# Mixture-of-experts layers in an eight-layer kernel: layer 2's rows dealt over the chunks, layer 1's weight halves issued earlier

## The chip, the cores and the metric

One core of one Trainium2 chip runs the whole program in one launch. The metric is the device time in microseconds (us). A run of this kernel is one execution of it; the time before is given as the median of three runs.

## The reference

Eight residual layers run over x of 8 x 256 tokens of 128 features: four pairs of a cross-attention and a feed-forward layer, each behind a layer norm. Two feed-forward layers matter here, and the text names them as the code does: "layer 1" (L = 3 in the code) and "layer 2" (L = 5).

```python
# layer 1: 64 experts of 88 hidden rows, 8 chosen per token, and a shared one
out = sum_e rw[t, e] * (silu(x @ gw_e.T) * (x @ uw_e.T)) @ dw_e.T
# layer 2: 8 experts, four 128 and four 256 rows wide, 2 chosen per token
probs = sigmoid(xf @ router_w.T)
topw, sel = top_k(probs, 2); topw = topw / (topw.sum(-1) + 1e-20)
h = square(relu(xf @ W1_e)); y_e = h @ W2_e
out = sum_e combine[t, e] * y_e
```

## The kernel before, in words

All 2048 tokens (16 tiles of 128, four groups q of 512) stay in SBUF. Five engines work side by side: PE (TensorE), DVE (VectorE), ACT (ScalarE), POOL (GpSimd), and SP, which only issues loads. Each has its own list of instructions in the order of the code. They wait for one another on semaphores, and a wait holds all that stands behind it on its engine.

**Two halves.** A matrix product of the expert layers runs in the fp32r format, which keeps fewer bits than f32. So every operand is split: ACT copies the f32 value into an fp32r high half, and POOL (or DVE) subtracts it from the f32 value into a low half. A product is then three matmuls (`product`, L1754 through `mm`): high by high, and the two crossed ones.

**Layer 1.** Its 5632 hidden rows are 44 chunks of 128, each with 8 rows of 16 experts. A unit is one chunk for one token group: 176 units. Unit n on PE is `gate_up1(n)` (6 matmuls) and `down1(n-3)` (3 matmuls). ACT does the silu (L1018) and the high half of the hidden rows (L791), DVE the two multiplications (L1552, L1557), POOL the low half (`hidden1_low`, L646). The weights of the next chunk are split once in four units: high halves by ACT (`gate_up1_high` behind s % 4 == 1, `down1_high` behind s % 4 == 2), low halves by POOL (`gate_up1_low` L638 at s % 4 == 2, behind `hidden1_low(s-1)`; `down1_low` L642 at s % 4 == 3). PE waits on `wgu_lo` ahead of the first unit of a chunk. The loads of raw weights wait for the low half that frees their buffer.

**Layer 2.** Its 1536 hidden rows are 12 chunks of 128, each belonging to one expert. The tokens are taken in two halves (hf) of 1024: 12 chunks for two groups, and then the same 12 chunks again, 48 units in all. So the weights of every chunk are split twice. A chunk belongs to a single expert, but each token has its own combine weight for it. PE therefore forms with `rows2` (one bf16 matmul by the selector `sel2` on `cT`, the combine weights split in three bf16 parts) a tile of that weight in PSUM beside each unit. In unit n PE does `up2` (3 matmuls), `rows2` (1) and `down2` (3) of the unit three earlier. ACT does the relu (L1105) and the high half; DVE does u2 = weight row x relu (L1659, PSUM by SBUF), h2 = u2 x relu (L1663, SBUF by SBUF) and the last 128 columns of the low half (L1670, `low2`), POOL the other 384 columns (L682) and the weights' low halves (L673, L677).

**Ahead of layer 2's units** PE forms the router's logits behind the transposes of the normed tokens. ACT takes the sigmoid (L1090) and then writes the high halves of the tokens (`norm_high`), POOL their low halves (`norm_low`, L614). DVE first does `integer_weights` (for the last layer), then finds every expert's rank among 8 by comparing all pairs (`rank_of`, L1483 to L1487, on 1024 elements), masks, normalises and splits the weights (L1642 to L1653). PE transposes them (L2226), ACT copies the result to `cT`. **Behind the units** ACT waits for all `down2`, copies the four sums (`o2T`), PE transposes them (L2268), and DVE adds them to X (L1275) and starts the next norm.

## Time and profile before

| what | value |
| --- | --- |
| median of three runs | 1149.82 us (1143.99, 1149.82, 1149.83) |
| the profiled execution's own time | 1143.57 us |
| its span, first to last instruction | 1141.8 us |
| mean granted TensorE clock | 0.921 |
| DMA, whole span | 23.02 MB, 20 GB/s on average |
| chain that ended last, by engine | PE 66%, DVE 19%, POOL 7%, issue 4%, ACT 4% |

The granted clock is 1.0 at 2.4 GHz and 0.5 at 1.2 GHz. Loads are small and far from any limit. PE carries most of the chain, but the eight layers have different limits, so each stretch is read by itself: layer 1's units run from about 450 to 818 us of the span, layer 2's routing from 882 to 898 us, and its units from 899 to 1012 us.

### The profile page before, as it was taken

To read this page: it belongs to the slowest core of one execution; us is meant where nothing else is said; L and a number is where in the kernel's file an instruction comes from. 1 tells how busy PE (TensorE), PEld (TensorE's weight loads), DVE (VectorE), ACT (ScalarE), POOL (GpSimd) and SP (SyncE) were. 2 spreads that over 40 slices of the span, in tenths; PEclk is the share of its full clock that TensorE was granted. 3 is DMA by queue.
4 is the path that set the end of the run, shared out by engine and by line. 5 is a ranking of instruction groups with operands and counts; after the bars stand their busy time and mean duration, and the time that the engine had idled before them with its cause. 6 is when DMAs were issued, how large, how long until landed. Compare 5 with 4: busy or idle time off the path is not lost.

```text
span 1141.8 us, 16173 instructions
## 1 busy us (share of the span) xinstructions
PE 974.2 (85%) x4525; PEld 716.0 (63%) x4525; DVE 778.8 (68%) x1598; ACT 584.3 (51%) x1145; POOL 536.4 (47%) x544
## 2 busy tenths in 40 slices
PE   5799899989998886999999999999966687857465
PEld 3577566657677644877777777777646444435244
DVE  7676455555534686666666666667568899976896
ACT  2344566665532254665656656566413455532584
POOL 6011322223303002777777777777555688763300
PEclk9899899999999898999999999999976699989576
DMA  5000000003200000000000000000010000000001
GB/s 166 1 1 1 1 1 1 1 25 101 78 10 24 1 1 12 24 22 28 21 24 25 21 25 23 21 28 21 0 61 1 1 1 0 1 0 1 0 8 30
DMA packets 27107, 23.02 MB, mean 20 GB/s; under 512 B 3419, under 2 KB 24115, under 8 KB 26931
## 3 DMA queue, kind: packets, MB, share of 16 engines
q1 hardware_dynamic: 27059, 22.43, 6.7%
q8 instruction: 24, 0.39, 0.1%
q14 instruction: 24, 0.20, 0.1%
HBM read 21.37 MB, written 1.05 MB: 20 GB/s over the span
## 4 chain that ended last, share of the span: by engine, by line
PE 66%; DVE 19%; POOL 7%; issue 4%; ACT 4%; DMA 0%; SPq 0%; POOLq 0%; ACTq 0%; DVEq 0%
PE psum L1754 59%; POOL hh L682 2%; DVE stats L1231 1%; PE psum L1875 1%; DVE xn L1244 1%; PE psum L1883 1%; DVE arena L1663 1%; PE psum L1823 1%; POOL rstd L594 1%; POOL wgu L673 1%; DVE arena L1307 1%; POOL xall L614 1%; POOL wdn L677 1%; DVE arena L1659 1%; DVE mv L1234 1%
## 5 line engine op out<-in xcount | busy, mean ns | idle before, releaser
L1754 PE MATMUL psum<-xall,wgu 128*128 128x512 f32 x1424 | 394.5, 411 | 27.6 <-POOL wgu L673 11.1
L1754 PEld LDWEIGHTS psum<-xall,wgu 128*128 128x128 f32 x1424 | 268.9, 193 | 114.0 <-issue 49.8
L646 POOL TENSOR_TENSOR hh<-arena,hh 128x512 fp32r<-128x512 f32 x176 | 227.7, 1294 | 107.1 <-ACT hh L791 105.0
L1754 PE MATMUL psum<-hh,wdn 128*128 128x512 f32 x672 | 197.0, 402 | 22.1 <-DVE hh L1670 22.1
L1552 DVE TENSOR_TENSOR psum<-psum,arena 128x512 f32<-128x512 f32 x176 | 123.0, 699 | 111.0 <-PE psum L1754 102.3
L1018 ACT ACTIVATE arena<-psum 128x512 f32<-128x512 f32 x176 | 105.3, 598 | 143.5 <-PE psum L1754 143.5
L791 ACT ACTIVATE hh<-arena 128x512 fp32r<-128x512 f32 x224 | 140.7, 628 | 50.9 <-DVE arena L1663 47.5
L1754 PEld LDWEIGHTS psum<-hh,wdn 128*128 128x128 f32 x672 | 123.6, 190 | 60.0 <-DVE hh L1670 23.3
L1754 PE MATMUL psum<-arena 128*128 128x18 f32 (+7 forms) x816 | 137.0, 318 | 5.7 <-DVE X L1634 3.5
L1557 DVE TENSOR_TENSOR arena<-psum,arena 128x512 f32<-128x512 f32 x176 | 121.7, 691 | 7.5 <-DVE psum L1552 1.7
L791 ACT ACTIVATE arena<-psum 128x1024 f32<-128x1024 f32 (+8 forms) x114 | 77.4, 691 | 96.4 <-PE psum L1754 31.9
L1754 PEld LDWEIGHTS psum<-arena 128*128 128x128 f32 (+3 forms) x816 | 97.5, 186 | 30.5 <-issue 26.6
L594 POOL TENSOR_TENSOR rstd<-veps,neghalf 128x4 f32<-128x4 f32 x24 | 24.3, 1014 | 108.4 <-DVE veps L1237 108.1
L747 POOL TENSOR_TENSOR arena<-arena 128x512 f32<-128x512 f32 x32 | 33.3, 1041 | 83.7 <-DVE arena L1359 83.6
L682 POOL TENSOR_TENSOR hh<-arena,hh 128x384 fp32r<-128x384 f32 x48 | 49.4, 1028 | 23.3 <-ACT hh L791 23.2
L1663 DVE TENSOR_TENSOR arena<-arena 128x512 f32<-128x512 f32 x48 | 57.2, 1191 | 3.4 <-DVE arena L1659 2.1
L618 POOL TENSOR_TENSOR wgu<-egu,wgu 128x256 fp32r<-128x256 f32 x32 | 24.0, 751 | 56.6 <-ACT wgu L791 56.6
L1772 PE MATMUL psum<-ident,xn 128*128 128x128 f32 x112 | 26.5, 396 | 26.5 <-POOL xn L600 13.5
L1404 DVE SCALAR_TENSOR_TENSOR arena<-psum,ebias,arena 128x512 f32<-128x512 f32 x32 | 24.0, 751 | 32.6 <-PE psum L1754 31.6
L638 POOL TENSOR_TENSOR wgu<-egu,wgu 128x256 fp32r<-128x256 f32 x44 | 32.8, 746 | 28.2 <-DVE arena L1533 28.2
L791 ACT ACTIVATE xnT<-psum 128x512 f32<-128x512 f32 x24 | 14.3, 598 | 57.2 <-PE psum L1772 57.1
L859 ACT ACTIVATE arena<-psum,arena 128x256 f32<-128x256 f32 x64 | 29.8, 470 | 25.1 <-DVE arena L1352 24.3
(287 smaller groups left out, 1493.9 us busy)
## 6 DMA issues: line engine op xcount, KB each, us to landing
egu<-in_w SPq DMA_DIRECT2D x44, 128.0 KB, 2.0
egu<-in_egu SPq DMA_DIRECT2D x16, 256.0 KB, 2.8
edn<-in_w SPq DMA_DIRECT2D x44, 64.0 KB, 1.8
edn<-in_edn SPq DMA_DIRECT2D x16, 128.0 KB, 2.0
arena<-in_w SPq DMA_DIRECT2D x1, 1536.0 KB, 5.9
X<-in_x SPq DMA_DIRECT2D x4, 256.0 KB, 3.8
out<-X SPq DMA_DIRECT2D x4, 256.0 KB, 2.3
arena<-in_ctxTd SPq DMA_DIRECT2D x1, 512.0 KB, 5.1
```

Of the source, the lines that this page charges most:

```text
L594: pool.tensor_tensor(rstd[:, s], veps[:, s], neghalf[:, s], ALU.pow).then_inc(ln_rstd, 1)
L638: pool.tensor_tensor(wgu[:, slot, 1, :], w1gu(slot), wgu[:, slot, 0, :].bitcast(F32), ALU.subtract).then_inc(wgu_lo, 1)
L646: pool.tensor_tensor(hh[:, s % 4, 1, :], h1[:, s % 2, :], hh[:, s % 4, 0, :].bitcast(F32), ALU.subtract).then_inc(hh_lo, 1)
L682: pool.tensor_tensor(hidden2_part(k, 1)[:, r], h2[:, k % 2, r], hidden2_part(k, 0)[:, r].bitcast(F32), ALU.subtract).then_inc(hh_lo, 1)
L747: pool.tensor_tensor(qb[:, k % 2], qb[:, k % 2], wide(recB[:, k % 2].unsqueeze(2), 2, N), ALU.mult)\
L791: return act.activation(dst, src, ACT.Copy)
L859: last = act.activation(qb[:, k % 2, c, :], psum[:, k % 2, c * N:(c + 1) * N], ACT.Exp, bias=nmB[:, k % 2, c:c + 1], accum_out=sumB[:, k % ...
L1018: act.activation(sil[:, k, :], bank(k), ACT.Silu).then_inc(nl_done, 1)
L1552: dve.tensor_tensor(bank(2 + k), bank(2 + k), sil[:, k, :], ALU.mult).then_inc(prod_done, 1)
L1557: dve.tensor_tensor(h1[:, k, :], bank(2 + k), rwb[:, s // 4, own], ALU.mult).then_inc(hid_done, 1)
L1663: dve.tensor_tensor(h2[:, k, :], u2[:, k, :], r2[:, k, :], ALU.mult).then_inc(hid_done, 1)
L1754: return pe.matmul(dst, lhsT=lhsT, rhs=rhs, start=start, stop=stop)
```

## The change: what it does

- **Layer 1.** ACT's `gate_up1_high` moves from behind s % 4 == 1 to behind s % 4 == 0; POOL's `gate_up1_low` moves from s % 4 == 2, behind `hidden1_low`, to s % 4 == 1, ahead of `hidden1_low`. The halves for the down product stay where they are.
- **Layer 2's rows** are dealt anew when the weights are laid out on the host: chunks 0 to 3 hold 32 rows of each of the four narrow experts, chunks 4 to 11 hold 32 rows of each of the four broad ones. So there are only two different tiles of combine weights over all tokens (`cB`). They are made once, by 8 matmuls and 8 copies; `rows2` goes.
- **All four token groups** pass through a chunk, in straight code in place of loops: 48 units again, but each chunk's weights are split once.
- **The hidden rows** take two scalar_tensor_tensor instructions on DVE, each with the unit's PSUM tile as one input: v2w = max(up, 0) x cB, h2 = max(up, 0) x v2w. ACT's relu and DVE's `low2` go; POOL makes all 512 columns of the low half. DVE does `weighted2(n+1)` ahead of `hidden2(n)`. In `down2` the matmul that needs the low half comes last, with a wait of its own.
- **Routing** uses max and match_replace, 16 of each, in place of the pairwise ranks; `integer_weights` comes behind it. The tokens' low halves go from POOL to DVE (`norm_low`, from PSUM), their high halves to just behind each group's transposes. Four groups of `up2` stand ahead of the combine weights on PE.
- **The end**: ACT copies a group's sum as soon as that group's last `down2` is done. Also, the selector tile shrinks from 12 to 2, a memset on POOL and a second load of chunk 0 go.

The core of the diff (`NC2` is 12, `NG` 4, `UNITS2` 48):

```diff
         taken[0] = 0
         pr2 = carve(NT, E2)
-        g2a = carve(NT, 8, 8)
-        g2b = carve(NT, 8, 8)
-        rank2 = carve(NT, 8)
+        best2 = carve(NT, 8)
+        rest2 = carve(NT, E2)
+        cw2 = carve(NT, E2)
         rs2 = carve(2, NT)
-        cpk = carve(NT, P, dt=BF16)
+        cpk = carve(NT, 3 * E2, dt=BF16)
         cT = carve(T, dt=BF16)
-        r2 = carve(2, 512)
-        u2 = carve(2, 512)
+        cB = carve(2, T)
+        v2w = carve(3, 512)
         h2 = carve(2, 512)
         o2T = carve(T)
...
                 def chunk_group(j, last=False):
                     for s in range(4 * RG):
+                        ahead = s // 4 + 1
+                        weights = not (last and ahead == RG)
+                        if s % 4 == 1 and weights:
+                            gate_up1_low(j * RG + ahead, ahead % 2)
                         if later(j, 1) or s:
                             hidden1_low(j * (4 * RG) + (s - 1), s - 1)
-                        ahead = s // 4 + 1
-                        if last and ahead == RG:
-                            continue
-                        if s % 4 == 2:
-                            gate_up1_low(j * RG + ahead, ahead % 2)
-                        if s % 4 == 3:
+                        if s % 4 == 3 and weights:
                             down1_low(j * RG + ahead, ahead % 2)
...
+            def hidden2_low(n):
+                pool.wait_ge(hh_hi, DONE1 + n + 1)
+                pool.tensor_tensor(hh[:, n % 4, 1, :], h2[:, n % 2, :], hh[:, n % 4, 0, :].bitcast(F32), ALU.subtract).then_inc(hh_lo, 1)
...
+                for c in range(2):
+                    up2_low(c)
+                    down2_low(c)
+                for n in range(UNITS2):
+                    c, s = n // NG, n % NG
+                    hidden2_low(n)
+                    if 1 <= c < NC2 - 1:
+                        if s == 0:
+                            up2_low(c + 1)
+                        if s == 2:
+                            down2_low(c + 1)
...
                     if later(j, 1) or s >= 2:
                         silu1(j * (4 * RG) + s, s % 2)
+                    ahead = s // 4 + 1
+                    weights = not (last and ahead == RG)
                     if later(j, 1) or s:
                         hidden1_high(j * (4 * RG) + (s - 1), s - 1)
-                    ahead = s // 4 + 1
-                    if last and ahead == RG:
-                        continue
-                    if s % 4 == 1:
+                    if s % 4 == 0 and weights:
                         gate_up1_high(j * RG + ahead, ahead % 2, j * (8 * RG) + (8 * E0 + 16 * (ahead // 2) + 16))
-                    if s % 4 == 2:
+                    if s % 4 == 2 and weights:
                         down1_high(j * RG + ahead, ahead % 2, j * (8 * RG) + (8 * E0 + 16 * (ahead // 2) + 16))
...
-            ln_evac(5)
+            for g in range(NG):
+                r = slice(512 * g, 512 * g + 512)
+                act.wait_ge(ln_tp, NG * 5 + g + 1)
+                copy(xnT[:, r], bank(LN_BANKS[5][g])).then_inc(ln_xnT, 1)
+                copy(norm_half(g, 0), bank(LN_BANKS[5][g])).then_inc(xh_hi, 1)
...
+            for k in range(4):
+                act.wait_ge(rb_mm, NG * RG + 2 * k + 1)
+                copy(cB[:, k // 2, 1024 * (k % 2):1024 * (k % 2) + 512], bank(4 + 2 * (k % 2))).then_inc(rb_sb[0], 1)
+            for n in range(UNITS2):
+                c, s = n // NG, n % NG
+                hidden2_high(n)
+                if 1 <= c < NC2 - 1:
+                    if s == 0:
+                        up2_high(c + 1)
+                    if s == 2:
+                        down2_high(c + 1)
             for q in range(NG):
+                act.wait_ge(down_done, DONE1 + UNITS2 - NG + q + 1)
...
+            for g in range(NG):
+                norm_low(5, g)
+            dve.wait_ge(rl_sig, 3)
+            for t in range(NT):
+                last = dve.max(best2[:, t, :], pr2[:, t, :])
+            then(last)
+            dve.tensor_tensor(rs2[:, 0, :], best2[:, :, 0], best2[:, :, 1], ALU.add)
+            then(dve.memset(best2[:, :, 2:8], 3.0e38))
+            dve.tensor_scalar(rs2[:, 0, :], rs2[:, 0, :], 1e-20, None, ALU.add)
+            for t in range(NT):
+                last = dve.match_replace(rest2[:, t, :], best2[:, t, :], pr2[:, t, :], -3.0e38)
+            then(last)
+            dve.tensor_tensor(rest2, pr2, rest2, ALU.not_equal)
+            then(dve.reciprocal(rs2[:, 1, :], rs2[:, 0, :]))
+            then(dve.tensor_tensor(cw2, rest2, pr2, ALU.mult))
+            then(dve.tensor_tensor(cw2, cw2, wide(rs2[:, 1, :].unsqueeze(2), NT, E2), ALU.mult))
+            then(dve.tensor_copy(cpk[:, :, 0:E2], cw2))
+            then(dve.tensor_tensor(cw2, cw2, cpk[:, :, 0:E2], ALU.subtract))
+            then(dve.tensor_copy(cpk[:, :, E2:2 * E2], cw2))
+            then(dve.tensor_tensor(cw2, cw2, cpk[:, :, E2:2 * E2], ALU.subtract))
+            dve.tensor_copy(cpk[:, :, 2 * E2:3 * E2], cw2).then_inc(rw_done, 1)
             integer_weights()
-            dve.wait_ge(rl_sig, 3)
...
-            def hidden2(n, s, first):
-
-                k = s % 2
-                dve.wait_ge(nl_done, n + 1)
-                dve.tensor_tensor(u2[:, k, :], bank(2 + k), r2[:, k, :], ALU.mult).then_inc(prod_done, 1)
-                dve.wait_ge(prod_done, n + 1)
-                dve.wait_ge(hh_hi, n - 1)
-                dve.wait_ge(hh_lo, n - 1)
-                dve.tensor_tensor(h2[:, k, :], u2[:, k, :], r2[:, k, :], ALU.mult).then_inc(hid_done, 1)
-                if not first:
-                    low2(n - 1, (s - 1) % 4)
-
-            def low2(n, k):
-                r = slice(LOW2, 512)
-                dve.wait_ge(hh_hi, n + 1)
-                dve.tensor_tensor(hidden2_part(k, 1)[:, r], h2[:, k % 2, r], hidden2_part(k, 0)[:, r].bitcast(F32), ALU.subtract).then_inc(hh_lo2, 1)
...
+            for k in range(4):
+                dve.wait_ge(rb_mm, NG * RG + 2 * k + 2)
+                dve.tensor_copy(cB[:, k // 2, 1024 * (k % 2) + 512:1024 * (k % 2) + 1024], bank(5 + 2 * (k % 2))).then_inc(rb_sb[1], 1)
+            for k in range(2):
+                dve.wait_ge(rb_sb[k], 2 * RG + 4)
+
+            def weighted2(n):
+                dve.wait_ge(up_ready, DONE1 + n + 1)
+                if n >= 3:
+                    dve.wait_ge(hid_done, DONE1 + n - 2)
+                q = n % NG
+                dve.scalar_tensor_tensor(v2w[:, n % 3, :], bank(q), 0.0, cB[:, 0 if n < 4 * NG else 1, 512 * q:512 * q + 512], ALU.max, ALU.mult)\
+                    .then_inc(prod_done, 1)
+
+            def hidden2(n):
+                dve.wait_ge(prod_done, DONE1 + n + 1)
+                if n >= 2:
+                    dve.wait_ge(hh_hi, DONE1 + n - 1)
+                    dve.wait_ge(hh_lo, DONE1 + n - 1)
+                dve.scalar_tensor_tensor(h2[:, n % 2, :], bank(n % NG), 0.0, v2w[:, n % 3, :], ALU.max, ALU.mult).then_inc(hid_done, 1)
+
+            weighted2(0)
+            for n in range(UNITS2):
+                if n + 1 < UNITS2:
+                    weighted2(n + 1)
+                hidden2(n)
             output_groups(6, NG)
...
-            def rows2(local, k, hf):
-
-                mm(bank(2 + k), sel2[:, bass.ds(local, 1), :].rearrange("p a n -> p (a n)"),
-                   cT[:, 1024 * hf + 512 * k:1024 * hf + 512 * k + 512]).then_inc(up_ready, 1)
...
+            def up2(n):
+                c, q = n // NG, n % NG
+                if q == 0:
+                    pe.wait_ge(wgu_lo, STEPS0 + NC1 + c + 1)
+                if n >= 4:
+                    pe.wait_ge(hid_done, DONE1 + n - 3)
+                else:
+                    pe.wait_ge(xh_lo, E0 + NG + q + 1)
+                if n == 0:
+                    pe.wait_ge(rl_sig, 3)
+                product(bank(q), lambda h: wgu[:, c % 2, h, 0:P], lambda h: norm_half(q, h)).then_inc(up_ready, 1)
+
+            def down2(n):
+                c, q = n // NG, n % NG
+                if q == 0:
+                    pe.wait_ge(wdn_lo, NC1 + c + 1)
+                pe.wait_ge(hh_hi, DONE1 + n + 1)
+                mm(bank(4 + q), wdn[:, c % 2, 1, :], hh[:, n % 4, 0, :], c == 0, False)
+                mm(bank(4 + q), wdn[:, c % 2, 0, :], hh[:, n % 4, 0, :], False, False)
+                pe.wait_ge(hh_lo, DONE1 + n + 1)
+                mm(bank(4 + q), wdn[:, c % 2, 0, :], hh[:, n % 4, 1, :], False, c == NC2 - 1).then_inc(down_done, 1)
+
...
+                for k in range(2 * NG):
+                    e, q = k // NG, k % NG
+                    if e:
+                        pe.wait_ge(rb_sb[q % 2], 2 * RG + q // 2 + 1)
+                    mm(bank(4 + q), sel2[0:3 * E2, e, :], cT[0:3 * E2, 512 * q:512 * q + 512]).then_inc(rb_mm, 1)
+                for q in range(2):
+                    pe.wait_ge(rb_sb[q], 2 * RG + 4)
+
+            for n in range(UNITS2 + 3):
+                if n < UNITS2:
+                    up2(n)
+                if n == 3:
+                    combine_rows2()
+                if n >= 3:
+                    down2(n - 3)
             for g in range(NG):
...
+    narrow = np.arange(4 * 128).reshape(4, 4, P // 4).transpose(1, 0, 2)
+    broad = 4 * 128 + np.arange(4 * 256).reshape(4, 8, P // 4).transpose(1, 0, 2)
+    dealt = np.concatenate([narrow.reshape(-1), broad.reshape(-1)])
+    w2 = np.concatenate([v["L2_ffn_w1"][:, dealt].reshape(D, NC2, P).transpose(1, 0, 2), v["L2_ffn_w2"][dealt].reshape(NC2, P, D)], axis=2).transpose(1, 0, 2)
```

## Rows read from the trace of the kernel before

**Rows 1.** The page: busy time of each engine over the span.
```profile
PE 974.2 (85%) x4525; PEld 716.0 (63%) x4525; DVE 778.8 (68%) x1598; ACT 584.3 (51%) x1145; POOL 536.4 (47%) x544
```
**Rows 2.** Windows view: start:end, length, busy us of each engine (instructions), granted clock, DMA.
```profile
455.00:816.00 361.00, 361.00 (x1544) 286.24 (x1544) 243.42 (x350) 217.62 (x427) 271.11 (x257) 1.00 0.08 23
...
899.00:1012.00 113.00, 90.17 (x326) 54.76 (x327) 107.98 (x144) 62.46 (x142) 88.56 (x95) 0.97 0.00 1
```
**Rows 3.** Timeline of PE, layer 1: start, us, line, operation, count.
```profile
560.04 1.52 PE L1754 MATMUL psum<-xall,wgu 128*128 128x512 f32 x6
...
562.08 1.52 PE L1754 MATMUL psum<-xall,wgu 128*128 128x512 f32 x6
...
564.25 1.65 PE L1754 MATMUL psum<-xall,wgu 128*128 128x512 f32 x6
...
572.68 0.49 PE L1754 MATMUL psum<-xall,wgu 128*128 128x512 f32 x1
```
**Rows 4.** Timeline of all engines, layer 1, around 564 us.
```profile
563.37 0.75 POOL L638 TENSOR_TENSOR wgu<-egu,wgu 128x256 fp32r<-128x256 f32 x1
```
**Rows 5.** Timeline, start of layer 1's second chunk; in brackets the idle time before it.
```profile
454.81 0.50 PE L1754 MATMUL psum<-xall,wgu 128*128 128x512 f32 x1 [0.99 <-POOL wgu L638]
```
**Rows 6.** Groups by shape, 900 to 1010 us (layer 2): busy us, mean ns, idle before.
```profile
L1663 DVE TENSOR_TENSOR arena<-arena 128x512 f32<-128x512 f32 x48 | 57.2, 1191 | 3.4 <-DVE arena L1659 2.1
L682 POOL TENSOR_TENSOR hh<-arena,hh 128x384 fp32r<-128x384 f32 x47 | 48.2, 1026 | 22.0 <-ACT hh L791 21.9
...
L1659 DVE TENSOR_TENSOR arena<-psum,arena 128x512 f32<-128x512 f32 x47 | 31.9, 678 | 0.0
...
L1670 DVE TENSOR_TENSOR hh<-arena,hh 128x128 fp32r<-128x128 f32 x47 | 25.3, 539 | 0.0
```
**Rows 7.** Groups by shape, 500 to 800 us (layer 1).
```profile
L646 POOL TENSOR_TENSOR hh<-arena,hh 128x512 fp32r<-128x512 f32 x143 | 185.1, 1294 | 76.1 <-ACT hh L791 74.6
...
L1552 DVE TENSOR_TENSOR psum<-psum,arena 128x512 f32<-128x512 f32 x143 | 100.0, 699 | 93.8 <-PE psum L1754 86.3 <-ACT arena L1018 7.5
...
L791 ACT ACTIVATE hh<-arena 128x512 fp32r<-128x512 f32 x143 | 89.7, 627 | 0.0
...
L642 POOL TENSOR_TENSOR wdn<-edn,wdn 128x128 fp32r<-128x128 f32 x35 | 16.8, 480 | 0.0
```
**Rows 8.** Two lines with scalar_tensor_tensor, by source: ns min/median/max, first and last start.
```profile
L1404 DVE SCALAR_TENSOR_TENSOR arena<-psum,ebias,arena x32: 749/751/754, 248.9 to 323.2; 128x512 f32<-128x512 f32 x32
...
L1705 DVE SCALAR_TENSOR_TENSOR arena<-arena,cols x16: 751/752/1411, 1071.6 to 1116.9; 128x512 f32<-128x512 f32 x16
```
**Rows 9.** Timeline of all engines, layer 2's routing.
```profile
881.78 0.28 ACT L1090 ACTIVATE arena<-psum 128x128 f32<-128x128 f32 x1 [2.67 <-PE psum L1754]
...
891.72 2.90 PE L1754 MATMUL psum<-xall,wgu 128*128 128x512 f32 x6 [10.03 <-POOL wgu L673]
...
893.90 0.29 DVE L1652 TENSOR_TENSOR arena<-arena 128x128 f32<-128x128 f32 x1
...
894.51 1.89 PE L2226 MATMUL psum<-identb,arena 128*128 128x128 bf16 x16
895.58 1.94 ACT L791 ACTIVATE arena<-psum 128x1024 bf16<-128x1024 bf16 x2 [11.24 <-PE psum L2226]
...
898.85 0.69 DVE L1659 TENSOR_TENSOR arena<-psum,arena 128x512 f32<-128x512 f32 x1 [4.40 <-ACT arena L1105]
```
**Rows 10.** Timeline of DVE, layer 1's routing.
```profile
416.67 1.19 DVE L1510 MAX8 arena<-arena 128x8 f32<-128x8 f32 x16
...
418.08 0.09 DVE L1514 MATCH_VALUE_LOAD arena<-arena 128x8 f32 x1
...
420.19 0.15 DVE L1514 MATCH_REPLACE8 arena<-arena 128x8 f32<-128x8 f32 x1
```
**Rows 11.** Timeline of all engines, end of layer 2's units.
```profile
1010.62 1.11 POOL L682 TENSOR_TENSOR hh<-arena,hh 128x384 fp32r<-128x384 f32 x1 [1.29 <-ACT hh L791]
...
1014.89 0.69 DVE L1275 TENSOR_TENSOR X<-psum,X 128x512 f32<-128x512 f32 x1 [4.02 <-PE psum L2268]
```

More of the change, by code:

```diff
@@ L1476, in _ @@
                 norm_behind(3, t)
-            def rank_of(dst, v, a, b2, n):
-                own = wide(v.unsqueeze(3), n, 8, 8)
-                other = wide(v.unsqueeze(2), n, 8, 8)
-                dve.tensor_tensor(b2, other, own, ALU.is_equal)
-                then(dve.tensor_tensor(a, other, own, ALU.is_gt))
-                then(dve.tensor_tensor(b2, b2, wide(ltmask[:, :, :].unsqueeze(1), n, 8, 8), ALU.mult))
-                then(dve.tensor_tensor(a, a, b2, ALU.add))
-                then(dve.tensor_reduce(dst, a, AX.X, ALU.add))
             def routing():
@@ L1763, in ln_transpose @@
                 pe.wait_ge(ln_xn, NG * L + g + 1)
-                if g >= 2:
+                into = LN_BANKS[L][g] if L in LN_BANKS else 6 + g % 2
+                if g >= 2 and L not in LN_BANKS:
                     pe.wait_ge(ln_xnT, NG * L + g - 1)
```

223 lines of the change are left out of this document (51 added, 172 removed).

## The prediction

> **What bounds the kernel now.** I read the page first: PE is busy 85% of the span, DVE 68% [rows 1]. That is an average over eight layers, so the windows view comes next, one window per stretch that the change touches. In layer 1's units PE is busy 361.00 of 361 us: PE is the bound. In layer 2's units it is DVE, busy 107.98 of 113 us, with PE at 90.17 and the clock at 0.97 [rows 2].
>
> Then the two stretches from near. In layer 1 a unit of nine matmuls usually takes 562.08 - 560.04 = 2.04 us, 0.227 us each. From 564.25 to 572.68 are four units: 8.43 us, where four times 2.04 are 8.16. The first unit of a chunk is late: it starts at 564.25, where 562.08 + 2.04 is 564.12 [rows 3]. POOL's low half of that chunk's weights ended at 563.37 + 0.75 = 564.12 [rows 4]. So PE waits for it, and loses 0.13 us in the wait and as much again in the matmuls behind it. In layer 2, DVE's three instructions per unit take 0.68 + 1.19 + 0.54 = 2.41 us, overlapping a little: 48 units need 112 us. Two of the three have both inputs in SBUF; the 512-column one takes 1.19 us, while the one that reads PSUM takes 0.68 for as many columns [rows 6]. DVE is what orders the unit: PE and ACT wait for it.
>
> **Layer 1, the weight halves.** The instructions are the same; only their places change. ACT issues the high half one unit sooner, and POOL issues the low half ahead of a hidden half instead of behind it and one unit sooner, so it ends about two units (4 us) before PE wants it. What could be late next is that hidden half: it now stands behind 0.75 us of weights. But those come while ACT's high half of the hidden rows isn't there yet, and POOL sits idle 76.1 of 300 us waiting for it [rows 7]; PE uses it three units later. The reload of the raw weights is freed earlier too, no later. So all of 8.43 - 8.16 = 0.27 us goes, at 42 chunk starts: 11 us. At the second chunk, PE's idle 0.99 us for the same weights goes too [rows 5]. Sum: **-12 us**; at the least 0 (the wait moves), at the most 12.5.
>
> **Layer 2, one unit after.** PE: 6 matmuls, 6 x 0.227 = 1.36 us. DVE: two scalar_tensor_tensor on 512 columns with a PSUM input. This form with an immediate scalar isn't in the trace. Its bounds are the tensor_tensor with a PSUM input, 0.70 [rows 7], and the scalar_tensor_tensor with a pointer scalar, 0.75 [rows 8]. So 1.40 to 1.50 us. ACT: 0.63 for the high half [rows 7], and small weight copies. POOL: 1.29 for 512 columns, and per chunk two weight halves at 0.48 [rows 7]: (4 x 1.29 + 2 x 0.48)/4 = 1.53 us. I don't take the slower POOL price of now (1.03 for 384 columns; the weights' 128 columns too are slower beside DVE's SBUF by SBUF instructions [rows 6]): line 646 has one duration throughout, next to DVE instructions that read PSUM.
>
> The engines are then close together, so the loop of waits counts. Say POOL ends low(n-3) at 0. The last matmul of down2(n-3) can start 0.23 later: in rows 3 and 4 that's the time from POOL's end to the first matmul that runs at the usual spacing (564.12 to 564.35). Then `up2(n+1)` has to follow in PE's order: three steps of 0.227, and 0.43 from the last start to the DVE start (a matmul's 0.39 and the semaphore): 1.34. DVE: weighted2(n+1) takes 0.65 until hidden2(n) starts, and that ends 0.70 later: 2.69. ACT 0.04 + 0.63, POOL 0.07 + 1.29: low(n) ends at 4.72. That is three units: 1.57 us each. With one weight half and one hidden half of POOL in the loop it is (4.72 + 1.29 + 0.48)/4 = 1.62; with DVE at 0.75 an eighth of a microsecond more goes into each round, 1.65. I take **1.64 us per unit**. Ends: 1.53 (POOL alone) and 1.80 (each of some three hand-overs per round slower by 0.15 us).
>
> **Layer 2, ahead of the units.** Now 17.1 us pass from the sigmoid at 881.78 to DVE's first unit at 898.85 [rows 9]. After: DVE's four token low halves (4 x 0.69 = 2.8 us) stand ahead of the sigmoid in the place of `integer_weights`, six instructions of the same width; the sigmoid's time is set by PE's router matmuls. From 882.1: 16 max 1.2 us; match_replace 0.137 us per tile (418.08 to 420.34 for 16), 2.3 us [rows 10]; some twelve small instructions at about 0.3 [rows 9] 3.4 us. The weights are ready at 888.9, where they now are at 894.5. `integer_weights` lies behind that, under PE's transposes and ACT's copies. The transposes and ACT's copies stay: 894.51 to 897.52, 3.0 us [rows 9], so `cT` stands at 892. New: 8 broadcast matmuls and 8 copies, four each on ACT and DVE, which alternate at 0.65 us: about 4 us with the first matmul at the low clock. DVE's first unit comes at 896.1: **-2.7 us**. PE meanwhile does up2 of four groups, 12 matmuls at 0.43 (six took 2.90 [rows 9]), 5.1 us from about 883 on: hidden.
>
> **The units.** Now: 898.85 to POOL's last half at 1011.73 [rows 9, 11], 112.9 us. After: low(0) ends 4.1 us behind DVE's first instruction; 46 units at 1.64 are 75.4; the last, with nothing behind it, 1.3; and 1.5 for matmuls at the lower clock until PE is warm, as now. Sum 82.3: **-30.6 us**. **The end:** now 3.16 us from POOL's last half to the first add into X [rows 11]. After, three of the four sums are already copied: some 1.3, **-1.9 us**. POOL's shorter selector and the memset that goes lie where it waits: 0.
>
> **Sum.** 12 + 2.7 + 30.6 + 1.9 = 47.2 us less. Against the profiled execution's own time, 1143.57: 1096.4 us. Of the three runs, one lies next to that time and two 6 us above it, so I put the forecast a little higher, at **1098 us**.
>
> **A rule against a measurement.** Of DVE beside POOL the rows say this: scalar_tensor_tensor with a PSUM input took 749 to 754 ns in all 32 cases, and the one with two SBUF inputs took 1411 once, against 752 [rows 8]; that once lay beside a POOL instruction. The Trainium skill (SBUF — State Buffer, "Who interferes with whom") says that a DVE instruction with at most one SBUF input doesn't contend with GpSimd, and one with two does when GpSimd reads SBUF. By that rule, the trace agrees. The skill's page on VectorE: DVE Perf Modes, on the other hand, gives an fp32 tensor_tensor (N + 151)/0.96, 691 ns here; with that for the new form as an estimate, the unit would come to 1.62.
>
> **Rivals.**
> - *PE loses its clock* (chance 0.04). PE would now pause in every round for POOL's half. At 0.427 us per matmul a unit costs 6 x 0.427 = 2.56 us, 48 x 0.92 = 44 us more than I forecast: 1142 us, no change. Against it: now PE pauses more (80% busy) and the clock stays up [rows 2]. The Trainium skill (TensorE: Matmul & The Clock Gate) tells of a kernel whose short idle times between groups of matmuls made the clock oscillate; here the granted clock doesn't show that.
> - *Layer 1's stall only moves* (0.08), say to the hidden half behind the weights: 1098 + 11 = 1109 us. For it: POOL has four instructions in a row there. Against it: POOL's idle time and the three units of distance.
> - *The loop in layer 2 is slower* (0.10): double-buffered `h2` and a semaphore at each step; with 2.0 us a unit 1098 + 47 x 0.36 = 1115 us.
> - *DVE and POOL exclude each other* (0.02), the one that ends slower. Each unit would cost 1.45 + 1.53 = 2.98 us, 48 x 1.34 = 64 us more: 1162 us, against 1143.6. It decides from about 2.8 us a unit on: then the loss of 48 x 0.47 = 22 us eats the 16.6 us won elsewhere and 5.7 more. Against it: rows 7 and 8.
> - *The change doesn't do what it says* (0.01): some wait keeps layer 2's groups in the old order; 1131 us from layer 1 alone.
>
> **How the numbers follow.** The forecast has 0.75. Its own range is 1.53 to 1.80 us a unit, -5 to +8 us, with 6 us of difference between runs: 1090 to 1110. With the next two rivals it reaches to 1115; below, DVE and PE in full step and layer 2's routing 3 us shorter give 1086. Range 1086 to 1115. A measurement of this kernel tells about 0.5% (5.7 us) from no change. Faster by more than that: 0.95; within it: 0.03, the clock's case; slower: 0.02.
>
> **What would show it.** In the profile after, layer 1's chunk takes 8.16 us, with no wait for the weights' low half. Layer 2's units take 79 us instead of 113, DVE's two lines 0.70 to 0.75 us each, POOL's low half 1.29, and DVE is busy about 88%, POOL 93%. PE's wait in `down2` is for POOL's half. The granted clock stays at 1.0. I am wrong if the unit takes over 1.8 us, if DVE's instructions are over 0.8 us, or if layer 1 keeps its 8.43.

## The result and the profile after

The kernel after takes **1088.83 us** (median of 4 runs, 1087.94 to 1094.18); the kernel before, on the same chip, 1146.90 (4 runs, 1141.13 to 1149.83). The ratio is 0.951, 95% interval 0.947 to 0.956: faster by 5%. The forecast was 1098, range 1086 to 1115. The profiled execution of after took 1088.47 us (span 1086.3), against 1143.57 (span 1141.8) before: 55.1 us less, where the sum of the prediction had 47.2.

I divided both spans at the same events and took the differences (us). "Product" in the table is the first of DVE's two multiplications of a layer 1 unit (L1552 before, L1499 after), not a matrix product; "last half" is the end of POOL's last low half.

| stage | before | after | difference | predicted |
|---|---|---|---|---|
| layer 1, first to last product | 367.38 | 354.84 | -12.54 | -12 |
| last product to first add into X | 12.11 | 12.08 | 0 | 0 |
| first add into X to attention's first add | 32.33 | 30.83 | -1.5 | 0 |
| attention's first add to the sigmoid | 20.69 | 19.62 | -1.1 | 0 |
| sigmoid to DVE's first unit of layer 2 | 17.07 | 13.76 | -3.3 | -2.7 |
| layer 2's units, to POOL's last half | 112.88 | 78.53 | -34.35 | -30.6 |
| POOL's last half to the first add into X | 3.16 | 1.11 | -2.05 | -1.9 |
| from there to the end | 126.92 | 127.15 | +0.2 | 0 |

Layer 1's first product came 0.9 us earlier as well, which no part of the change touches; in the profiles of this kernel and its variants it comes anywhere between 447.8 and 452.1 us. So single runs are compared by stages below, not by their totals.

The page of after, busy time and instructions of each engine (before: [rows 1]):

```profile
PE 950.2 (87%) x4485; PEld 716.7 (66%) x4485; DVE 728.9 (67%) x1602; ACT 557.3 (51%) x1077; POOL 502.8 (46%) x512
```
The windows of after over layer 1's units and within layer 2's (before: [rows 2]):

```profile
450.00:812.00 362.00, 360.26 (x1575) 295.52 (x1576) 249.54 (x358) 222.31 (x436) 276.23 (x261) 1.00 0.08 23
890.00:955.00 65.00, 64.21 (x246) 42.67 (x244) 53.07 (x83) 29.90 (x61) 61.27 (x62) 1.00 0.00 1
```
Layer 1 is still PE's. In layer 2 DVE, which was busy 96% and set the unit, is now at 82% (53.07 of 65); POOL is at 94% and PE at 99%. The forecast had 88% for DVE and 93% for POOL.

Layer 1, timeline of PE and POOL after, where chunks start at 550.70 and 558.86 (before: [rows 3] and [rows 4]):

```profile
548.66 1.52 PE L1710 MATMUL psum<-xall,wgu 128*128 128x512 f32 x6
...
550.70 1.52 PE L1710 MATMUL psum<-xall,wgu 128*128 128x512 f32 x6
...
558.86 1.52 PE L1710 MATMUL psum<-xall,wgu 128*128 128x512 f32 x6
```
```profile
545.94 0.75 POOL L624 TENSOR_TENSOR wgu<-egu,wgu 128x256 fp32r<-128x256 f32 x1
546.65 1.29 POOL L632 TENSOR_TENSOR hh<-arena,hh 128x512 fp32r<-128x512 f32 x1
...
554.03 0.75 POOL L624 TENSOR_TENSOR wgu<-egu,wgu 128x256 fp32r<-128x256 f32 x1
```
Every unit is 2.04 us after the last, the first of a chunk too: 550.70 - 548.66 = 2.04 and 558.86 - 550.70 = 8.16. The low half ends at 546.69, 4.0 us or two units ahead of its use at 550.70; the hidden half stands right behind it, and makes nobody wait.

Layer 2, groups by shape from 890 to 955 us of after (before: [rows 6]), and the waits of the same stretch (who waits for whom: us in total, times, longest):

```profile
L666 POOL TENSOR_TENSOR hh<-arena,hh 128x512 fp32r<-128x512 f32 x42 | 54.4, 1295 | 4.3 <-ACT hh L762 3.6
L1627 DVE SCALAR_TENSOR_TENSOR arena<-psum,arena 128x512 f32<-128x512 f32 x42 | 28.6, 681 | 0.2 <-DVE arena L1619 0.2
L1619 DVE SCALAR_TENSOR_TENSOR arena<-psum,arena 128x512 f32<-128x512 f32 x41 | 28.4, 692 | 11.5 <-PE psum L1710 11.0
...
L658 POOL TENSOR_TENSOR wgu<-arena,wgu 128x128 fp32r<-128x128 f32 x10 | 4.6, 462 | 0.0
```
```profile
ACT hh L762 <- DVE arena L1627: 35.5, 42, 1.1
PEld psum L1710 <- POOL hh L666: 12.4, 40, 0.6
DVE arena L1619 <- PE psum L1710: 11.0, 36, 0.6
POOL hh L666 <- ACT hh L762: 3.6, 17, 0.6
```
Read the waits as a ring. In nearly every unit PE's weight load for the last matmul of `down2` waits for POOL, DVE for PE, ACT for DVE; POOL waits for ACT in 17 of 42. The unit is 1.574 us long (mean of 32, from the ninth start of line 1619 on). Of that POOL works (4 x 1.295 + 2 x 0.462)/4 = 1.53 us, DVE 1.37, and PE's six matmuls of 0.227 need 1.36. PE's busy time shows more: the ends of matmuls are modelled in this profile, and one of `down2` is given 421 ns on the mean, one of layer 1 389.

The routing after (before: [rows 9]), timeline:

```profile
865.73 0.28 ACT L1060 ACTIVATE arena<-psum 128x128 f32<-128x128 f32 x1 [2.19 <-PE psum L1710]
...
866.04 1.19 DVE L1590 MAX8 arena<-arena 128x8 f32<-128x8 f32 x16 [1.77 <-ACT arena L1060]
...
872.60 0.23 DVE L1606 CAST arena<-arena 128x128 bf16<-128x128 f32 x1
...
873.54 1.92 ACT L762 ACTIVATE arena<-psum 24x1024 bf16<-24x1024 bf16 x2 [6.74 <-PE psum L2184]
...
879.49 1.29 DVE L1619 SCALAR_TENSOR_TENSOR arena<-psum,arena 128x512 f32<-128x512 f32 x2
```
The weights are ready 7.1 us behind the sigmoid (forecast 7.1), `cT` 9.7 (10.2), DVE's first unit 13.8 (14.3).

### The profile page after: what moved, and what is told of

It reads as the page before. It is cut to its first block, busy times and chain, and to the rows that moved or that the text cites. A ratio compares the mean times of both kernels' runs of the same rounds, so it can differ in the third digit from the quotient of the medians.

```text
span 1086.3 us, 15531 instructions
## 1 busy us (share of the span) xinstructions
PE 950.2 (87%) x4485; PEld 716.7 (66%) x4485; DVE 728.9 (67%) x1602; ACT 557.3 (51%) x1077; POOL 502.8 (46%) x512
## 4 chain that ended last, share of the span: by engine, by line
PE 73%; DVE 17%; POOL 3%; ACT 3%; issue 2%; DMA 0%; SPq 0%; DVEq 0%; ACTq 0%
PE psum L1710 66%; DVE stats L1189 1%; PE psum L1832 1%; PE psum L1840 1%; PE psum L1780 1%; POOL rstd L586 1%; DVE xn L1202 1%; DVE arena L1265 1%; POOL hh L666 1%; PE psum L1729 1%; DVE mv L1192 1%; PE psum L1903 1%; DVE arena L1660 1%; DVE arena L1661 1%; DVE arena L1667 1%
## 5 line engine op out<-in xcount | busy, mean ns | idle before, releaser
L1710 PEld LDWEIGHTS psum<-xall,wgu 128*128 128x128 f32 x1424 | 272.7, 194 | 88.2 <-issue 25.6
L632 POOL TENSOR_TENSOR hh<-arena,hh 128x512 fp32r<-128x512 f32 x176 | 227.9, 1295 | 81.4 <-ACT hh L762 80.1
L1499 DVE TENSOR_TENSOR psum<-psum,arena 128x512 f32<-128x512 f32 x176 | 123.0, 699 | 98.4 <-PE psum L1710 92.1
L1710 PEld LDWEIGHTS psum<-hh,wdn 128*128 128x128 f32 x672 | 126.5, 189 | 45.9 <-POOL hh L666 16.1
L1710 PE MATMUL psum<-arena 128*128 128x18 f32 (+7 forms) x776 | 122.0, 317 | 5.3 <-DVE X L1581 2.6
L762 ACT ACTIVATE arena<-psum 128x1024 f32<-128x1024 f32 (+9 forms) x118 | 79.7, 687 | 90.4 <-PE psum L1710 30.1
L1710 PEld LDWEIGHTS psum<-arena 128*128 128x128 f32 (+3 forms) x776 | 95.0, 193 | 18.8 <-issue 14.8
L666 POOL TENSOR_TENSOR hh<-arena,hh 128x512 fp32r<-128x512 f32 x48 | 61.9, 1293 | 20.4 <-ACT hh L762 19.7
L1619 DVE SCALAR_TENSOR_TENSOR arena<-psum,arena 128x512 f32<-128x512 f32 x48 | 33.1, 691 | 13.6 <-PE psum L1710 12.9
L762 ACT ACTIVATE xnT<-psum 128x512 f32<-128x512 f32 x24 | 14.3, 598 | 53.4 <-PE psum L1729 53.3
```

The costliest lines, as they stand in the source:

```text
L632: pool.tensor_tensor(hh[:, s % 4, 1, :], h1[:, s % 2, :], hh[:, s % 4, 0, :].bitcast(F32), ALU.subtract).then_inc(hh_lo, 1)
L666: pool.tensor_tensor(hh[:, n % 4, 1, :], h2[:, n % 2, :], hh[:, n % 4, 0, :].bitcast(F32), ALU.subtract).then_inc(hh_lo, 1)
L762: return act.activation(dst, src, ACT.Copy)
L1499: dve.tensor_tensor(bank(2 + k), bank(2 + k), sil[:, k, :], ALU.mult).then_inc(prod_done, 1)
L1619: dve.scalar_tensor_tensor(v2w[:, n % 3, :], bank(q), 0.0, cB[:, 0 if n < 4 * NG else 1, 512 * q:512 * q + 512], ALU.max, ALU.mult)\
L1710: return pe.matmul(dst, lhsT=lhsT, rhs=rhs, start=start, stop=stop)
```

## Experiments

**Layer 1's part alone.** The kernel before, with two orders changed:

```diff
+                        if s % 4 == 1 and weights:
+                            gate_up1_low(j * RG + ahead, ahead % 2)
                         if later(j, 1) or s:
                             hidden1_low(j * (4 * RG) + (s - 1), s - 1)
-                        if s % 4 == 2:
-                            gate_up1_low(j * RG + ahead, ahead % 2)
...
-                    if s % 4 == 1:
+                    if s % 4 == 0 and weights:
                         gate_up1_high(...)
```


> The kernel before with only layer 1's two orders changed (ACT's and POOL's weight halves one unit sooner, POOL's ahead of the hidden half); layer 2 as before. My theory (the 0.27 us at each chunk start go, and nothing else of layer 1 is touched): layer 1 from its first product to its last takes 354.8 us instead of 367.4, a chunk 8.16 instead of 8.43, layer 2's stages keep their times, and the run is 12.5 us shorter than the kernel before (ratio 0.989). Rival (a part of layer 1's gain depends on what else changed, the rest moves to a later wait): a chunk over 8.2 us or a gain under 10 us.

Measured: 1131.26 us (4 runs) against 1142.17, ratio 0.989 (0.984 to 0.993). That is under 2%, but clear of no change. Layer 1 takes 354.82 us, a chunk 8.16. The other stages of the table keep their times within 0.6 us; what lies ahead of layer 1's first product, where nothing was changed, was 2.8 us longer in the profiled run. The gain is layer 1's and needs nothing else.

**Only ACT's half of it.** `if s % 4 == 1` becomes `if s % 4 == 0` for the high half on ACT; POOL's order stays.

> The kernel before with only ACT's high half of layer 1's gate and up weights one unit sooner; POOL's low half stays where it was, behind the hidden half. My theory (what is late is POOL's low half by its place in POOL's order, not for want of its input): POOL's instruction starts where it did, and a chunk keeps 8.43 us; the gain is under 1 us. Rival (ACT's place was what held it): 8.16 us and 12 us less.

Measured: one run, 1143.91 us; layer 1 takes 367.35 us. POOL's low half and PE's next unit, in the timelines of POOL and of PE, and then, from the kernel before, ACT's high half of the same chunk's weights:

```profile
563.66 0.75 POOL L638 TENSOR_TENSOR wgu<-egu,wgu 128x256 fp32r<-128x256 f32 x1
```
```profile
562.37 1.52 PE L1754 MATMUL psum<-xall,wgu 128*128 128x512 f32 x6
...
564.54 1.65 PE L1754 MATMUL psum<-xall,wgu 128*128 128x512 f32 x6
```
```profile
559.90 0.41 ACT L791 ACTIVATE wgu<-egu 128x256 fp32r<-128x256 f32 x1
```
POOL ends at 564.41, PE starts 0.13 us behind it and 2.17 behind its unit before: the pattern of [rows 3] and [rows 4]. So ACT's move by itself gains nothing. In the kernel before, ACT's half was ready at 560.31, and POOL began its own at 563.37 [rows 4], straight behind a hidden half: what held it was its place in POOL's order. Whether POOL's move alone, with ACT's left out, would have won all 12.5 us no run shows; by these times POOL's input would have been there in time.

**POOL's removed work given back.** After, plus the old selector and the old memset on tiles that nobody reads:

```diff
+                    then(pool.memset(idle_sel, 0.0))
+                    for part in range(3):
+                        then(pool.affine_select(out=idle_sel[:, 0:4, :], ...))
+                        then(pool.affine_select(out=idle_wide, ...))
...
+                    pool.memset(idle_pk, 0.0).then_inc(pool_step, 1)
                     experts2_low()
```


> The changed kernel with the work that POOL no longer does given back, on tiles that nobody reads: the memset of 128 x 1536 and the six selections of the old selector ahead of layer 2's attention, and the memset of 128 x 2048 after it. The prediction priced their removal at 0. By it: no stage changes. By the theory formed from the two profiles (DVE's layer-norm instructions run slower while POOL writes memory beside them): the stage from layer 1's first add into X to attention's first takes 32.3 us again instead of 30.8, attention's first add to the sigmoid 20.7 instead of 19.6, the eight layer-norm instructions there 4.4 us instead of 2.5 and the four 2.4 instead of 1.1; together 2.6 us more. Layer 2's units keep 1.57 us each.

Measured: one run, 1090.39 us. The two stages take 31.82 and 20.69 us: +1.0 and +1.1. DVE's layer-norm line of after, then the same line with POOL's work beside it, then that work and the second stretch again by single instructions (ns: least, median, most; in after 336, 339, 345):

```profile
825.03 2.50 DVE L1202 TENSOR_SCALAR xn<-X,mv,rstd 128x128 f32<-128x128 f32 x8 [0.98 <-POOL rstd L586]
859.94 1.11 DVE L1202 TENSOR_SCALAR xn<-X,mv,rstd 128x128 f32<-128x128 f32 x4 [1.12 <-POOL rstd L586]
```
```profile
825.96 4.39 DVE L1214 TENSOR_SCALAR xn<-X,mv,rstd 128x128 f32<-128x128 f32 x8 [0.98 <-POOL rstd L589]
861.87 2.37 DVE L1214 TENSOR_SCALAR xn<-X,mv,rstd 128x128 f32<-128x128 f32 x4 [1.12 <-POOL rstd L589]
```
```profile
826.85 1.38 POOL L745 MEMSET arena<- 128x1536 bf16 x1
...
861.78 1.80 POOL L763 MEMSET arena<- 128x2048 bf16 x1
```
```profile
L1214 DVE TENSOR_SCALAR xn<-X,mv,rstd x4: 329/968/1796, 861.9 to 863.9; 128x128 f32<-128x128 f32 x4
```
These are DVE instructions with one SBUF tensor as input, and a memset reads nothing. They don't all get slower: of the four in the second stretch, the two that begin while the memset runs last until it ends, 1.80 and 1.60 us instead of 0.34, and the other two keep their time. In the first stretch the memset holds two so (1.57 and 1.38 us), and the selections behind it two more (0.80 and 1.08). So 2.1 us of the 2.6 unforeseen in these two stages are this; the other 0.5 us also went with layer 1's part alone (31.79 instead of 32.33), where POOL's work is the old one. I did not isolate it; the granted clock rose and fell at other moments of that stage in the two.

**The pairwise ranking given back.** After, with `rank_of` and its masks in place of max and match_replace.

> The changed kernel with the old pairwise comparison of the eight experts in place of max and match_replace; the order of the work around it, the masks and the units stay new. In the profile before, the weights were ready 12.4 us behind DVE's start on them (882.09 to 894.45), five wide instructions taking 9.1 of it; after the change 6.8 us (866.04 to 872.83). My theory (the routing gains by its fewer and smaller instructions, and pays for it with the broadcast rows): the stage from the sigmoid to DVE's first unit is 5.6 us longer, 19.3 us instead of 13.8, the run that much slower. Rival (before, POOL's token halves beside them slowed these five, which read two SBUF inputs; without POOL there they take their short times): 1.2 us each, only 2 to 3 us longer.

Measured: one run, 1094.65 us; sigmoid to DVE's first unit 17.5 us, +3.8: between the two. Its third wide instruction and a POOL instruction that it met; then, from the kernel before, the same instruction at 2.17 us and POOL's work beside it:

```profile
870.78 1.44 POOL L665 TENSOR_TENSOR wdn<-arena,wdn 128x128 fp32r<-128x128 f32 x1
871.93 1.37 DVE L1446 TENSOR_TENSOR arena<-arena,ltmask 128x1024 f32<-128x1024 f32 x1
```
```profile
882.66 8.39 POOL L614 TENSOR_TENSOR xall<-xnT,xall 128x512 fp32r<-128x512 f32 x4 [6.00 <-ACT xall L791]
...
885.56 2.17 DVE L1485 TENSOR_TENSOR arena<-arena,ltmask 128x1024 f32<-128x1024 f32 x1
```
The five wide instructions take 6.7 us here and took 9.1 before. POOL's small weight halves beside them wait in turn: four took 1.23 to 1.44 us instead of 0.46. So some 2.4 us of the routing's gain came from moving the token halves off POOL and 3.8 from the new instructions; of these 6.2 the stage kept 3.3, and the rest went into what the change adds there, the broadcast rows above all: from `cT` to DVE's first unit 4.0 us pass after, and 1.3 before.

**What sets layer 2's unit: four kernels.** First `down2` one unit later in PE's order (`range(UNITS2 + 4)`, `if n >= 4: down2(n - 4)`).

> The changed kernel with down2 one unit later in PE's order (up2(n), then down2(n - 4) instead of n - 3). My theory (the unit of 1.57 us is set by the loop low(n-3), down2, up2(n+1), weighted2, hidden2, ACT, low(n): 4.7 us for three units): the loop now spans four units, 1.18 us each, and POOL's own work remains: (4 x 1.295 + 2 x 0.462)/4 = 1.53 us, POOL busy all of it; 1.7 us less in all. Rival 1 (POOL alone sets the unit already and 1.57 is its work with small gaps): 1.57 stays. Rival 2 (the waits of DVE on POOL through the two hidden buffers set it): 1.57 stays too, but POOL still has gaps behind ACT's copies.

Then the kernel after with POOL's low halves of the weights left out from the third chunk on; PE waits for `wgu_hi` and `wdn_hi` there and multiplies by the low halves of an earlier chunk, so this kernel serves for its times only.

> The changed kernel without POOL's low halves of layer 2's weights from the third chunk on (PE multiplies by the halves of two chunks earlier there; it waits for ACT's high halves instead). POOL's work falls from 1.53 to 1.30 us per unit. My theory (three units of lag: a loop of 4.6 us through POOL, PE, DVE, ACT and POOL again): the unit falls only to 1.54 us, at the least 1.47 (the time that two of the four units of a chunk have now). Rival (POOL's own work is the bound of the unit): 1.30 to 1.36 us, layer 2's units 10 us shorter.

And both:

> Both: down2 one unit later, and no low halves of the weights on POOL from the third chunk on. In the run with the later down2 the unit was 1.544 us, POOL's work 1.53. My theory: with both bounds moved the next is the pair of hidden buffers, hidden2(n) behind POOL's low(n-2): 0.07 + 0.69 + 0.04 + 0.63 + 0.07 + 1.30 = 2.80 us for two units, 1.40 us, beside DVE's own 1.37; so 1.40 to 1.43. Rival (PE: six matmuls of 0.227 are 1.36, and loads not hidden add to them): PE busy all the time and a unit over 1.45.

| kernel | POOL's own work | unit | DVE's first unit to POOL's last half |
|---|---|---|---|
| after | 1.53 | 1.574 | 78.53 |
| down2 later | 1.53 | 1.544 | 75.73 |
| no low weights | 1.30 | 1.532 | 77.11 |
| both | 1.30 | 1.436 | 71.87 |

POOL's share of work fell by 0.23 us and the unit by 0.04: POOL alone was no bound. With one more unit between the halves the unit meets POOL's own work, (4 x 1.301 + 2 x 0.462)/4 = 1.53, and POOL's waits for ACT nearly vanish. The two bounds lie 0.04 us apart, so moving one alone shortens the stage by 2.8 or 1.4 us, and moving both by 6.7. The waits of the three variants from 890 to 950 us, in that order, show the bound moving:

```profile
PEld psum L1710 <- POOL wgu L658: 7.7, 9, 0.9
...
POOL hh L666 <- ACT hh L762: 1.1, 5, 0.3
```
```profile
PEld psum L1705 <- POOL hh L666: 12.2, 38, 0.6
DVE arena L1614 <- PE psum L1705: 8.1, 25, 0.5
```
```profile
POOL hh L666 <- ACT hh L757: 6.2, 22, 0.6
DVE arena L1622 <- POOL hh L666: 5.6, 16, 0.9
```
In the second the ring of after is left as it was (PE for POOL in 38 units). In the third DVE waits for POOL through the two hidden buffers, as expected; its unit, 1.436, lies just above the 1.40 to 1.43 that this theory gave. These kernels tell what bounds the unit of after. What the single parts of the change are worth in layer 2 (the rows dealt anew, fewer instructions on DVE) they don't tell; no run gives the dealing of the rows back.

**The operands decide, not the form.** `hidden2` reads `v2w` twice instead of `bank(n % NG)` and `v2w`; it computes something else, and serves for its times only.

> The changed kernel with hidden2 reading the weighted hidden twice, from SBUF, instead of once from SBUF and once from PSUM (so the product isn't the reference's); sizes, waits and engines stay. It measures the rival that DVE and POOL exclude each other, which the change avoids by reading PSUM. By that rule DVE's instruction takes 1.2 to 1.4 us instead of 0.68 (rows of before: 1.19 mean beside POOL, 1.41 once), POOL's low half up to as much longer, and the unit 1.9 to 2.3 us instead of 1.57: 16 to 35 us more. If it isn't the operands but the instruction's form that decides, 0.68 and 1.57 stay.

Measured: one run, 1112.90 us; the unit is 2.066 us. Groups from 890 to 950 us, and DVE's line by single instructions over all units (ns: least, median, most):

```profile
L666 POOL TENSOR_TENSOR hh<-arena,hh 128x512 fp32r<-128x512 f32 x30 | 42.6, 1440 | 7.2 <-ACT hh L762 7.2
L1627 DVE SCALAR_TENSOR_TENSOR arena<-arena 128x512 f32<-128x512 f32 x30 | 34.7, 1156 | 8.6 <-POOL hh L666 8.6
```
```profile
L1627 DVE SCALAR_TENSOR_TENSOR arena<-arena x48: 673/994/1665, 881.8 to 978.4; 128x512 f32<-128x512 f32 x48
```
681 ns became 1156 on the mean by where one operand lies, and POOL's instruction grew from 1295 to 1440. The means hide two cases. The 24 of these instructions that begin while no POOL instruction runs take 0.67 or 0.68 us, as with PSUM; the 24 that begin while one runs take 1.31 to 1.66. So two SBUF inputs cost DVE nothing by themselves. The units and their end take 23.7 us more: a good half of what the change wins in layer 2 hangs on each unit instruction having one SBUF input.

**A better version, in two steps.** With POOL's work and the ring both in the way, POOL makes all low weight halves ahead of the units, ACT copies both halves at once, `down2` comes one unit later and `h2` has three buffers:

```diff
+    pool.tensor_tensor(w2x[:, a:b, 1, :], w2all[:, a:b, :], w2x[:, a:b, 0, :], ALU.subtract).then_inc(w2_lo, 1)
...
+    copy(wgu[:, c % 2, :, 0:P], w2x[:, c, :, 0:P]).then_inc(wgu_lo, 1)
+    copy(wdn[:, c % 2, :, :], w2x[:, c, :, P:2 * P]).then_inc(wdn_lo, 1)
```


> A version that may beat both: POOL makes the low halves of all twelve chunks' weights while DVE does layer 2's routing (seven instructions, 8 us, where POOL waits now); in the units ACT copies both halves of a chunk in one instruction; down2 one unit later; three hidden buffers instead of two. My theory: POOL 1.30, PE 1.36, DVE 1.37 us per unit, DVE is the bound with 1.39, 48 units are 8.6 us shorter; the start of the units is up to 1 us later for ACT's extra copies: about 1081 us against 1088.8 for the changed kernel (ratio to the kernel before 0.944 to 0.946). Rival 1 (DVE's small routing instructions are slowed by POOL beside them, as the layer norm was): 2 to 3 us of it lost, first DVE unit over 15.5 us behind the sigmoid instead of 13.8. Rival 2 (three engines at 94 to 99% don't fit in step): 1.45 us or more per unit, 1085 us.

Measured: 1082.48 us (6 runs, 1079.94 to 1090.49), ratio to before 0.944 (0.940 to 0.948). The unit fell to 1.360 us, below the 1.39 expected, but DVE's first unit came 16.5 us behind the sigmoid: rival 1 of the expectation. The routing on DVE beside POOL's `w2x`:

```profile
872.44 7.67 POOL L663 TENSOR_TENSOR arena<-arena 128x256 f32<-128x256 f32 x7 [6.55 <-ACT arena L756]
...
874.04 1.07 DVE L1598 TENSOR_SCALAR arena<-arena 128x16 f32<-128x16 f32 x1
...
877.89 1.08 DVE L1604 TENSOR_TENSOR arena<-arena 128x128 f32<-128x128 f32 x1
879.01 1.25 DVE L1605 TENSOR_TENSOR arena<-arena 128x128 f32<-128x128 f32 x1
```
Instructions of 0.3 us last until the POOL instruction that they met ends: the last began at 879.01 beside a POOL instruction that ended at 880.11, and ended at 880.26. The second step puts POOL's halves where DVE reads PSUM (behind layer norm's last instruction, five of seven) and behind the routing (two); and PE's wait at layer 1's end is split, which is also run by itself on the kernel after:

```diff
-            pe.wait_ge(hs_done, 2 * NG)
             for g in range(NG):
+                pe.wait_ge(hs_done, 2 * g + 2)
```


> The changed kernel with one wait of PE split at the end of layer 1: the shared experts' last matmuls wait for the hidden rows of their own group instead of for all eight, so PE starts them about 1.7 us sooner and has no idle time there but at the last group. Theory: the stage from the last product to the first add into X takes 10.4 us instead of 12.1, and the clock no longer falls there, so no run lies 6 us above the others; 1087 us median. Rival (the clock's fall doesn't depend on this idle time): 1087 for most runs and 1093 for some.

> The changed kernel as it is, again, to stand beside the next two on one chip. Profiles of it and of its variants differ in one stage alone that the edits don't touch: from layer 1's last product to the first add into X 12.1 us, but 18.8 in two of them, with the granted clock at 0.50 where the others show 1.00. My theory: that is why single runs differ by 6 to 7 us; its runs fall in two groups, about 1088 and 1094 us, the former more often.

> The version with POOL's weight halves ahead of the units, improved by what its profile showed: DVE's first unit came 16.5 us behind the sigmoid (13.8 without) since four of DVE's small routing instructions took 1.1 to 1.3 us instead of 0.3 beside POOL's. Now ACT makes the high halves right behind layer 2's attention, POOL five of its seven instructions before the sigmoid and two once the routing weights are done, and the split wait at layer 1's end is in as well. Theory: units 1.36 us each, first unit 13.8 to 14.2 us behind the sigmoid, 10.4 us at layer 1's end: 1075 to 1077 us in all runs, ratio to the kernel before 0.938 to 0.940. Rival (the contention only moves to DVE's layer-norm and integer instructions): first unit over 15 us behind the sigmoid or attention's end over 20.5 us, 1078 us or more.

Measured on one chip, 6 runs each:

| kernel | median us | lowest, highest | ratio to before, 95% |
|---|---|---|---|
| after, again | 1091.05 | 1087.24, 1095.46 | 0.951 (0.948 to 0.955) |
| after, wait split | 1086.20 | 1085.19, 1089.60 | 0.947 (0.944 to 0.951) |
| better version | 1075.61 | 1073.51, 1077.33 | 0.938 (0.934 to 0.941) |

The better version beats the kernel after by 15 us. Its unit is 1.36 us, and its window of the units says why it won't go lower this way:

```profile
885.00:940.00 55.00, 55.00 (x244) 45.53 (x244) 52.02 (x82) 31.95 (x61) 52.07 (x41) 1.00 0.00 1
```
PE is busy 55.00 of 55 us, and the unit is just six matmuls of 0.227, 1.36: PE issues without a gap, as in layer 1. I had expected DVE to be the last bound, at 1.39; its two instructions overlap a little (52.02 for 41 units, 1.27 each). The first unit comes 14.1 us behind the sigmoid.

## Why the prediction was right, and where its sum was short

**Layer 1: right.** -12.54 against -12; the chunk is 8.16 us, and the run with ACT's move alone, with the times at which its half was ready, bears out that POOL's place held PE. The hidden half behind the weights delays nobody.

**The bounds of the unit: right, its value a little high.** The forecast had a ring of 4.72 us for three units, 1.57 each, and then added "one weight half and one hidden half of POOL in the loop" to reach 1.62, and took 1.64. That addition was the step that failed. The unit is 1.574: the plain ring. Leaving the weight halves out moved it by 0.04 only, so they lie for the most part where POOL would wait for ACT. 46 x 0.066 = 3.0 of the 3.7 us missing in this term are that. DVE's price came out at the lower end of its bounds or just under it: 681 and 692 ns, about the tensor_tensor's price, not the 751 of [rows 8] with a pointer scalar.

**"POOL's shorter selector and the memset that goes lie where it waits: 0": wrong.** They lay there for POOL, but not for DVE beside it: 2.1 us. The step asked who waits for POOL's instructions, and not whose instructions run slower during them, though [rows 8] had shown one such case. The Trainium skill (SBUF — State Buffer, "Who interferes with whom") holds both halves of the answer: besides the rule on two SBUF inputs, which the prediction quoted, it says that tensor_scalar can enter a mode in which it takes the ports shared with GpSimd, and then one of the two blocks for the whole of the other's instruction. By that, the runs agree: eight of layer norm's went from 2.50 to 4.39 us, and a single one of 0.34 us lasted 1.80, until the memset ended. The section's sentence on at most one SBUF input holds, in its own words, "outside the 2-port perf modes"; the prediction had left this condition out.

**The routing and the end: right within 0.6 us.** The forecast built the new stage from its own instructions and subtracted it from the old one's time, so that it needed no price for what POOL's token halves had cost there (some 2.4 us). The weights came as forecast (7.1), the broadcast took 4.0 us for 4.1, and the half microsecond missing lies in the transposes and ACT's copies between them: 2.6 us for 3.0.

**The rivals.** PE kept its clock in the units (1.00 from 890 to 955 us). Layer 1's stall did not move. The loop was not slower than forecast but faster, 1.574 for 1.64. The exclusion of DVE and POOL is real, but the change avoids it by reading PSUM: the priced 2.98 us for full exclusion was too much even for the version that invites it (2.07): there only one of DVE's two instructions has two SBUF inputs, and every second one of these is held.

What the terms missed, in the order of the table: 0.5, 2.6, 0.6, 3.7 and 0.2, and 0.9 us at the start, less 0.2 at the end: 8.3. 47.2 + 8.3 = 55.5, the difference of the two spans.

**Where luck helped.** The measured time lies 2.8 us above the lower end of the range. That end was worked out from DVE and PE in full step and a routing 3 us shorter still, and neither came: what took the time down there was POOL's work beside DVE, which the sum had at 0, and the ring without its added halves. The 0.9 us at the start are no effect of the change either.

## What to carry to other kernels

When several engines are each 80 to 95% busy and each waits for the next, write down the ring of waits, divide its length by the number of units that it spans, and compare that with each engine's own work: the larger is the unit, and one more unit of lag is worth only what lies between it and the next bound. When work leaves GpSimd, look at the VectorE instructions that ran beside it, not only at who waited for it, and at single instructions, since a mean hides that one of them is held and the next is not. And put GpSimd's bulk work where VectorE reads PSUM.

## What the runs showed of the hardware

**One stretch has two lengths.** From layer 1's last product to the first add into X, 12.1 us in most profiles, took 18.8 in two (the later `down2`, and the first step of the better version), whose edits lie elsewhere. The windows of the kernel after, and then of the one with the later `down2`, show the granted clock (third number from the end):

```profile
804.00:806.00 2.00, 0.45 (x1) 0.30 (x2) 1.50 (x2) 0.63 (x1) 1.58 (x2) 1.00 0.00 0
806.00:808.00 2.00, 2.00 (x6) 0.95 (x5) 0.00 (x0) 0.42 (x1) 0.63 (x1) 1.00 0.00 0
808.00:810.00 2.00, 2.00 (x6) 0.81 (x5) 0.00 (x0) 0.17 (x1) 0.00 (x0) 1.00 0.00 0
```
```profile
804.00:806.00 2.00, 0.99 (x3) 0.52 (x4) 0.95 (x2) 0.63 (x1) 1.59 (x2) 1.00 0.00 0
806.00:808.00 2.00, 2.00 (x5) 0.72 (x4) 0.00 (x0) 0.60 (x1) 0.08 (x1) 0.64 0.00 0
808.00:810.00 2.00, 2.00 (x4) 0.95 (x3) 0.00 (x0) 0.00 (x0) 0.00 (x0) 0.50 0.00 0
```
In both PE had been busy throughout layer 1, waited 1.74 us for DVE's last shared hidden rows, and was busy again when the clock fell from 2.4 to 1.2 GHz in one of the two, and not in the other. The six runs of the kernel after on the last chip lie in two groups, 1087.2 to 1088.8 and 1093.3 to 1095.5, about as far apart as the two lengths of this stretch, and the mean granted clock of the upper three is lower (0.913 to 0.916, against 0.919 to 0.921). With the wait split PE has no idle time there (14.00 of 14 us busy from 801 us on; in the kernel after, 12.26 of 14 from 802 us on), the stretch takes 10.1 us, and the runs spread over 4.4 us instead of 8.2. That the upper group is this stretch is shown in profiles only for the two variants; two of the six runs with the split wait still lie about 3 us above the rest, at a lower mean clock too (0.916 and 0.915 against 0.920), and I did not find where.

**A GpSimd instruction that only writes holds VectorE's tensor_scalar until it ends**, as the memset showed: 1.80 us for 0.34. And a short VectorE tensor_tensor with two SBUF inputs that begins beside a GpSimd tensor_tensor lasts until that one ends: 1.25 us for 0.29, in the first step of the better version. In the same stretch MAX8, MATCH_REPLACE8 and RECIPROCAL kept their 0.15, 0.14 and 0.24 us. It works the other way too: with the pairwise ranking given back, GpSimd's small halves lasted 1.23 to 1.44 us for 0.46 beside VectorE's wide instructions.
